# Layer 1 of a recommendation tower: the second pair of fp32 matmuls replaced by three f32r passes, with ScalarE and GpSimd preparing the operands

## The reference

```python
e = jnp.stack([tbl_0[ids[:, 0]], ..., tbl_31[ids[:, 31]]], axis=1)   # (512, 32, 32)
x0 = prev = e
for W in (filter_0, filter_1):
    z = jnp.einsum('bhd,bmd->bhmd', x0, prev).reshape(b, h * m, d)
    cur = jax.nn.relu(jnp.einsum('bpd,pn->bnd', z, W[0]))            # 128 maps
    prev = cur
    outs.append(cur)
z = jnp.sum(jnp.concatenate(outs, axis=1), axis=-1)                  # (512, 256)
h = jnp.concatenate([z, dense_ctx], axis=1)
h = jnp.maximum(h @ W_top1 + b_top1, 0.0)
h = jnp.maximum(h @ W_top2 + b_top2, 0.0)
y = h @ W_top3
```

## Time and profile before

| | before |
|---|---|
| median of 3 runs | 865.25 us (864.55 to 865.81) |
| the profiled execution's own time | 865.07 us |
| span in its profile | 863.3 us |
| busy: TensorE, VectorE, ScalarE, GpSimd | 854.4, 778.2, 680.4, 655.3 us |
| two fp32 matmuls of layer 1 (L751), instructions | 132 |
| mean granted TensorE clock | 0.992 |

### The profile page before, as it was taken

One profiled execution on the slowest core, in us unless ns is written; L12 is line 12 of the kernel. 1 busy time (PEld: TensorE's weight loads), 2 busy tenths in 40 slices (PEclk: granted clock), 3 DMA queues, 4 the chain that ended last, 5 costly groups with the idle time before them and its releaser, 6 DMA issues.

```text
span 863.3 us, 13937 instructions
## 1 busy us (share of the span) xinstructions
PE 854.4 (99%) x3583; PEld 672.2 (78%) x3583; DVE 778.2 (90%) x2392; ACT 680.4 (79%) x2231; POOL 655.3 (76%) x677
## 2 busy tenths in 40 slices
PE   8999999999999999999999999999999999999998
PEld 3777787777778777777877777787777778777866
DVE  4889999999999999999999999999999999999952
ACT  3778888888888888888888888888888888888832
POOL 5577788888887888778788877778878878866740
PEclk9999999999999999999999999999999999999988
DMA  5878866668677666777666687766668776664500
GB/s 168 200 201 197 199 133 139 158 161 185 163 170 151 135 157 162 182 165 181 146 131 153 162 182 167 178 151 131 150 158 185 168 178 137 139 145 93 99 6 0
DMA packets 54949, 130.86 MB, mean 152 GB/s; under 512 B 8020, under 2 KB 18996, under 8 KB 54869
## 3 DMA queue, kind: packets, MB, share of 16 engines
q0 software_dynamic: 22240, 68.17, 42.9%
q1 hardware_dynamic: 31090, 59.13, 22.4%
q10 hardware_dynamic: 1539, 2.67, 0.9%
HBM read 59.69 MB, written 4.20 MB: 74 GB/s over the span
## 4 chain that ended last, share of the span: by engine, by line
PE 96%; DMA 2%; DVE 1%; POOL 0%; ACT 0%; issue 0%; SPq 0%; ACTq 0%
PE t_act L784 13%; PE t_act L786 13%; PE t_act L785 13%; PE t_dve L784 13%; PE t_dve L786 13%; PE t_dve L785 13%; PE acc L751 7%; PE acc L756 5%; PE t_act L794 1%; PE acc L760 1%; DMA x_rows<-emb 1%; PE t_dve L805 1%; PE t_dve L841 1%; PE t_act L862 0%; PE t_dve L855 0%; DVE prod L577 0%
## 5 line engine op out<-in xcount | busy, mean ns | idle before, releaser
L420 ACT ACTIVATE prod<-t_act,weigh 128x128 f32<-128x128 f32 x2048 | 576.5, 373 | 101.5 <-PE t_act L786 96.6
L577 DVE SCALAR_TENSOR_TENSOR prod<-t_dve,weigh,prod 128x128 f32<-128x128 f32 x1792 | 481.5, 342 | 9.4 <-PE t_dve L786 7.4
L303 POOL TENSOR_TENSOR prod<-prod 128x512 f32<-128x512 f32 (+1 forms) x255 | 296.8, 1164 | 19.6 <-DMA prod<-prod 8.8
L784 PE MATMUL t_act<-w_hi,cur_hi 128*128 128x512 f32 x512 | 212.3, 415 | 0.0
L786 PE MATMUL t_act<-w_hi,cur_lo 128*128 128x512 f32 x512 | 199.7, 390 | 0.0
L785 PE MATMUL t_act<-w_lo,cur_hi 128*128 128x512 f32 x512 | 199.6, 390 | 0.0
L784 PE MATMUL t_dve<-w_hi,cur_hi 128*128 128x512 f32 x512 | 199.5, 390 | 0.0
L786 PE MATMUL t_dve<-w_hi,cur_lo 128*128 128x512 f32 x512 | 199.3, 389 | 0.0
L785 PE MATMUL t_dve<-w_lo,cur_hi 128*128 128x512 f32 x512 | 199.1, 389 | 0.0
L283 POOL DMA_DIRECT2D prod<-prod x126 | 118.9, 944 | 104.6 <-ACT prod L420 63.2
L264 POOL DMA_INDIRECT emb<-table_dram,all_ids x128 | 163.8, 1279 | 40.0 <-issue 30.0
(11 more groups left out here) (93 smaller groups left out, 572.9 us busy)
## 6 DMA issues: line engine op xcount, KB each, us to landing
prod<-prod POOLq DMA_DIRECT2D x126, 512.0 KB, 5.1
x_shift<-x_rows SPq DMA_DIRECT2D x62, 512.0 KB, 5.9
x_pair<-x_rows SPq DMA_DIRECT2D x94, 128.0 KB, 4.3
x_same<-x_rows SPq DMA_DIRECT2D x31, 256.0 KB, 3.3
x_rows<-emb SPq DMA_DIRECT2D x64, 64.0 KB
w_raw<-w_dram ACTq DMA_DIRECT2D x8, 256.0 KB, 4.1
emb<-table_dram,all_ids POOLq DMA_INDIRECT x128, 2.9
w_raw<-wt_dram SPq DMA_DIRECT2D x2, 512.0 KB, 9.9
```

The costliest lines, as they stand in the source:

```text
L303: nc.gpsimd.tensor_tensor(src[:, dst, :], src[:, dst, :], src[:, other, :], ALU.add).then_inc(folded, 1)
L420: last = nc.scalar.activation(prod[i][:, HEADS * a + j, :], t_act[n % ARING][:, j * MAPS:(j + 1) * MAPS], ACT.Copy, scale=weigh[p][:, i, h ...
L577: nc.vector.scalar_tensor_tensor(dst, src, w, dst, ALU.mult, ALU.add).then_inc(added, 1)
L784: nc.tensor.matmul(bank[:, :], cur_hi[p][:, cols], w_hi[:, w], start=True, stop=False)
```

## The change

All four groups of layer 1 are done in three f32r passes from chunk 3 on (chunks 0 to 2 stay as they were). The z_hi, z_lo, v_hi and v_lo buffers have four groups in place of two. For the added groups 0 and 1, ScalarE rounds both in one activation (`round_first`), between `relu2` and tile 3, and `round_last` moves behind tile 3; GpSimd makes the two low parts (`lower_first`), between the fold of tile 1 and `halve` of tile 3. To make room in SBUF, the context input and its weights lie in `w_raw`, and the rounded halves of `pool1` in z_hi and z_lo. A semaphore counts the first half of each layer 1 (`layer1_half`), for which `round_first` waits; two more connect ScalarE, GpSimd and TensorE.

```diff
-SPLIT = 2
-WHOLE = GROUPS - SPLIT
+WHOLE = GROUPS // 2
...
-        z_hi = sb("z_hi", [128, SPLIT, COLS], f32r)
-        z_lo = sb("z_lo", [128, SPLIT, COLS], f32r)
+        z_hi = sb("z_hi", [128, GROUPS, COLS], f32r)
+        z_lo = sb("z_lo", [128, GROUPS, COLS], f32r)
...
-        v_hi = sb("v_hi", [128, SPLIT, MAPS], f32r)
-        v_lo = sb("v_lo", [128, SPLIT, MAPS], f32r)
+        v_hi = sb("v_hi", [128, GROUPS, MAPS], f32r)
+        v_lo = sb("v_lo", [128, GROUPS, MAPS], f32r)
...
-        ctx_sb = sb("ctx_sb", [CTX, BATCH])
-        wt1_ctx = sb("wt1_ctx", [CTX, TOP1])
...
+        room = 2 * TOP1 + T1 * TOP2
+        ctx_sb = w_raw[0:CTX, room:room + BATCH]
+        wt1_ctx = w_raw[0:CTX, room + BATCH:room + BATCH + TOP1]
...
-        pool1_hi, pool1_lo = (sb(f"pool1_{half}", [128, BATCH], f32r)[:, :] for half in ("hi", "lo"))
+        pool1_hi, pool1_lo = z_hi[:, 0, :], z_lo[:, 0, :]
...
+            def lower_first(c, p):
+                pool.wait_ge(first_rounded, c - LEAD + 1)
+                for g in range(WHOLE):
+                    nc.gpsimd.tensor_tensor(z_lo[:, g, :], z[p][:, g, :], z_hi[:, g, :].bitcast(fp32),
+                                            ALU.subtract).then_inc(first_lo_ready, 1)
...
+                    if i == 3 and 0 < c < CHUNKS - 2:
+                        lower_first(c + 2, p)
...
+            def round_first(c, p):
+
+                act.wait_ge(z_ready, c * 3 + 1)
+                act.wait_ge(layer1_half, c - 1)
+                nc.scalar.activation(z_hi[:, 0:WHOLE, :], z[p][:, 0:WHOLE, :], ACT.Copy).then_inc(first_rounded, 1)
...
-                    if i == 2 and not ((c == 0 or c + 2 >= CHUNKS)):
+                    if i == 2 and 0 < c < CHUNKS - 2:
+                        round_first(c + 2, p)
+                    if i == 3 and 0 < c < CHUNKS - 2:
                         round_last(c + 2, p)
...
-            nc.vector.tensor_copy(v_hi[:, :, :], v[:, WHOLE:GROUPS, :]).then_inc(v_ready, 1)
+            nc.vector.tensor_copy(v_hi[:, :, :], v[:, :, :]).then_inc(v_ready, 1)
...
-                    if g < WHOLE or g < GROUPS and c <= 2:
+                    if g < GROUPS and c < LEAD:
...
-                        nc.tensor.matmul(acc1[:, :], v[:, g, :], z[p][:, g, :], start=g == 0, stop=False)
+                        last = nc.tensor.matmul(acc1[:, :], v[:, g, :], z[p][:, g, :], start=g == 0, stop=False)
+                        if g == WHOLE - 1:
+                            last.then_inc(layer1_half, 1)
                     elif g < GROUPS:
-                        k = g - WHOLE
-                        pe.wait_ge(z_lo_ready, (c - 3) * SPLIT + k + 1)
-                        for weights, rows in ((v_hi, z_hi), (v_lo, z_hi), (v_hi, z_lo)):
-                            nc.tensor.matmul(acc1[:, :], weights[:, k, :], rows[:, k, :], start=False, stop=False)
+                        if g < WHOLE:
+                            pe.wait_ge(first_lo_ready, (c - LEAD) * WHOLE + g + 1)
+                        else:
+                            pe.wait_ge(z_lo_ready, (c - LEAD) * WHOLE + g - WHOLE + 1)
+                        nc.tensor.matmul(acc1[:, :], v_hi[:, g, :], z_hi[:, g, :], start=g == 0, stop=False)
+                        nc.tensor.matmul(acc1[:, :], v_lo[:, g, :], z_hi[:, g, :], start=False, stop=False)
+                        last = nc.tensor.matmul(acc1[:, :], v_hi[:, g, :], z_lo[:, g, :], start=False, stop=False)
+                        if g == WHOLE - 1:
+                            last.then_inc(layer1_half, 1)
```

More of the change, by code:

```diff
@@ L147, in dlrm_tower @@
         z_rounded = sem("z_rounded")
+        layer1_half, first_rounded, first_lo_ready = sem("layer1_half"), sem("first_rounded"), sem("first_lo_ready")
         pair_rounded, z_lo_ready = sem("pair_rounded"), sem("z_lo_ready")
@@ L235, in chunk @@
                 sp.dma_start(x_shift[p][:, WHOLE:GROUPS, :].rearrange("p g c -> p (g c)"),
-                             shifted(WHOLE, SPLIT)).then_inc(x_rest[p], 16)
+                             shifted(WHOLE, GROUPS - WHOLE)).then_inc(x_rest[p], 16)
             def top_loads():
@@ L396, in round_pair @@
                 act.wait_ge(layer1_done, c)
-                nc.scalar.activation(z_hi[:, :, :], z[p][:, WHOLE:GROUPS, :], ACT.Copy).then_inc(pair_rounded, 1)
+                nc.scalar.activation(z_hi[:, WHOLE:GROUPS, :], z[p][:, WHOLE:GROUPS, :], ACT.Copy).then_inc(pair_rounded, 1)
             def relu2(c, p):
@@ L528, in lower_pair @@
                 dve.wait_ge(pair_rounded, c - 2)
-                for k in range(SPLIT):
-                    nc.vector.tensor_tensor(z_lo[:, k, :], z[p][:, WHOLE + k, :], z_hi[:, k, :].bitcast(fp32),
+                for g in range(WHOLE, GROUPS):
+                    nc.vector.tensor_tensor(z_lo[:, g, :], z[p][:, g, :], z_hi[:, g, :].bitcast(fp32),
                                             ALU.subtract).then_inc(z_lo_ready, 1)
@@ L608, in _ @@
             dve.wait_ge(v_ready, 1)
-            nc.vector.tensor_copy(v_hi[:, :, :], v[:, WHOLE:GROUPS, :]).then_inc(v_ready, 1)
+            nc.vector.tensor_copy(v_hi[:, :, :], v[:, :, :]).then_inc(v_ready, 1)
             dve.wait_ge(v_ready, 2)
-            nc.vector.tensor_tensor(v_lo[:, :, :], v[:, WHOLE:GROUPS, :], v_hi[:, :, :].bitcast(fp32),
+            nc.vector.tensor_tensor(v_lo[:, :, :], v[:, :, :], v_hi[:, :, :].bitcast(fp32),
                                     ALU.subtract).then_inc(v_ready, 1)
```

## The result

| | before | after |
|---|---|---|
| median | 865.53 us (864.55 to 868.05, 4 runs) | 899.66 us (896.39 to 904.58, 4 runs) |
| the profiled execution's own time | 865.07 us | 899.89 us |
| span in its profile | 863.3 us | 898.1 us |
| busy: TensorE, VectorE, ScalarE, GpSimd | 854.4, 778.2, 680.4, 655.3 us | 857.8, 851.7, 699.1, 776.0 us |

The kernel became slower by the factor 1.0401 (95% interval 1.0358 to 1.0443). The forecast was 911 us, 11 us too much; the time lies in the range of 861 to 933. What follows gives the mechanism as forecast in the main, one of its two reasons refuted, and one engine that had not been counted.

A forecast was written before the change was run, and what follows sets the result against it. TensorE was taken as the bound, with GpSimd to become it: 28 periods of 26.86 instead of 25.14 us add 48.2, less 2.6 of lead, so 865.07 + 45.6 and 0.2 give 911 us; range 861 to 933.

The forecast's parts named there:

- TensorE's part: Layer 1's first half: six f32r passes replace the fp32 pair, 1.36 for 1.72 us, saving 0.36 us per chunk, 10.4 total.
- ScalarE, preamble, addresses at nothing: ScalarE's added 1.07 us rounding, moved round_last, larger v_hi and v_lo, and changed SBUF places were taken to cost nothing.
- it fits: Rival: GpSimd never falls behind and TensorE's saving of 0.36 to 0.41 us per chunk shows, 854.9 to 853.4 us; chance 0.12.
- The first reason, the chain through a landing: GpSimd's path from tile 3's DMA through tile 1's landing, fold and subtractions takes 25.1 us, over TensorE's 24.78.
- bound by the landing chain, but the collisions stay off: Rival: GpSimd's period is 25.1 us and the product stays in the second subtraction, 861.5 us; chance 0.06.
- The second reason, the collisions: VectorE's two-SBUF-input operations and GpSimd's tensor operations block each other, first the product in lower_first; 2.30 us per chunk.
- 24.56 + 2.30 = 26.86 us: GpSimd's period: 22.08 us without waits plus 2.48 for subtractions, then blocks of 1.13, 0.87 and 0.3 us.
- the lead that is used up first: GpSimd's 2.9 us ahead of TensorE's need for low parts, less 0.36, taken off the loss as 2.6 us.
- 28 equal periods: From chunk 3's layer 1 to chunk 31's, each period lengthens from 25.14 to 26.86 us, 48.2 us more.
- no wait of GpSimd for ScalarE or VectorE left: Sign expected in the profile after: GpSimd, late throughout, no longer waits for tiles from ScalarE or VectorE.
- the idle 2.48 us in which the product lay: GpSimd's wait before the DMA at 454.49, where VectorE's 1.13 us product at 453.86 ran and lower_first would stand.

The follow-up runs named there:

- the run with one-input products: Changed kernel with VectorE's three products per chunk replaced by transposes of one input, products left out of the computation: 853.66 us, ratio 0.9847 to the kernel before.
- one subtraction each: Changed kernel with GpSimd making only group 0's low part and VectorE group 1's, between tile 3 and the second product: 876.83 us, ratio 1.0126 to the kernel before.

## Why the prediction was right in its direction, and where it was wrong

**TensorE's part: right.** 0.36 us per chunk, or 0.41 with the slower passes behind the fp32 pair, were forecast; 0.41 was measured (24.73 against 25.14). In the run with one-input products the six passes take 1.36 us, as written. The change gets nothing of it, since TensorE no longer sets the pace.

**ScalarE, preamble, addresses at nothing: right.** The run without GpSimd's subtractions has all of them and ends at 855.77, with 855 forecast for "it fits". In the change the layer 1 of chunk 3 even starts 0.7 us earlier, not later.

**The first reason, the chain through a landing: wrong.** The step "that is 25.1 us around, over 24.78" took 444.13 - 429.36 = 14.77 us for GpSimd's work, and in these stood a gather of 2.11 us. 1.06 of it was a collision with the product beside it, so the chain is 24.0 us. The step should have asked why one gather of four takes twice as long as the others. The rival "bound by the landing chain, but the collisions stay off", 861.5 us, is not what comes without the products' collisions: the period is then TensorE's 24.73. The time of the other branch, "it fits" (854.9 to 853.4), is that of the run with one-input products (853.66). Its condition, a loss below 0.22 us per chunk, was too tight, since the gathers held by z_lo lose 1.1 us in ten chunks of that run, 0.4 per chunk, and cost nothing.

**The second reason, the collisions: right, and the whole of the loss.** Half of the place was wrong, though: the collision at the subtractions is the smaller part, 13.1 of the 46.0 us, and the first product and z_last against the folds are the larger. The product splits the subtraction pair as described, but from chunk 2 on. In chunk 1, where the prediction saw it already, the fold ended at 74.5 and not at the 75.74 of the kernel before, so the product was due in the second subtraction, was held itself, and GpSimd was spared. Both timelines of the change, GpSimd and then VectorE:

```profile
74.50 2.56 POOL L281 TENSOR_TENSOR z_lo<-z,z_hi 128x512 fp32r<-128x512 f32 x2
...
100.65 3.52 POOL L281 TENSOR_TENSOR z_lo<-z,z_hi 128x512 fp32r<-128x512 f32 x2
```

```profile
76.14 2.00 DVE L537 TENSOR_TENSOR z<-x_shift,x_same 128x1024 f32<-128x1024 f32 x1
...
101.24 1.78 DVE L537 TENSOR_TENSOR z<-x_shift,x_same 128x1024 f32<-128x1024 f32 x1
```

**The size: the sum was right by two errors that nearly cancel.** The forecast was 24.56 + 2.30 = 26.86 us for GpSimd's period. Measured, its work is 24.73 - 1.15 = 23.58 us in the chunk of the run with one-input products in which nothing is held, and the collisions are 3.53 - 2.55 = 1.0 in the subtractions, 4.21 - 2.55 = 1.7 in one fold and 2.91 - 2.55 = 0.4 in another, 3.0 in all: 26.6. The distance of the subtractions from 100.65 to 793.26 us, 26 chunks, gives 26.64. So 24.56 held a collision of 1.06 that the kernel before already had, and 2.30 was 0.7 too small: errors of about 1.0 and 0.7 us in opposite directions. That they nearly cancel is luck, and so is much of how close 911 comes. Over 28 periods, with the lead that is used up first, 45.6 us were forecast and 37.5 measured. The lead was right at the start: the low parts of chunk 3 are done at 77.06 us, 2.55 before TensorE starts on that layer 1. But at the end they are still 1.79 us ahead (819.25 against 821.04), so only 0.8 us of it went. What makes the 8.1 us is the period, 26 x 0.22 = 5.7, and its two ends: the first distance between two pairs of subtractions is 26.15 us, and the last, from 793.26 to 816.72, 23.45, since GpSimd has no gathers left in the last of these chunks. The sum had taken 28 equal periods. That is 0.7 + 3.4 + 5.7 - 1.8 = 8.0. The shorter stretches ahead of and behind the 28 periods make the other 2.7 us.

**VectorE: not foreseen.** The prediction counted a collision as a loss of GpSimd's. VectorE loses as much: in the chunk shown cur_lo 1.80, the second product 0.61 and the two z_lo 0.61 us, 3.0 us in all. On average over the 26 chunks VectorE's two-input operations lose 3.2 us per chunk, and GpSimd's subtractions and folds 2.9. VectorE is full at 26.5 of 26.76. The kernel before had 1.4 us of idle time in VectorE's period, less than half of that. TensorE's stall on t_dve banks, 22.6 us in all, is VectorE's lateness. The profile was to show "no wait of GpSimd for ScalarE or VectorE left", and from 95 to 800 us it has one such wait before the DMA of L290, of 0.9 us, and six short ones before gathers, 1.3 us in all: the sign came true there. The other 18 us of the two lines of the waits lie in the first and the last chunks.

**What "it fits" lacked.** Its chance of 0.12 rested on a sum of busy times. Single collisions in the trace before and the idle 2.48 us in which the product lay were what spoke against it, and they did decide.

## What to carry to other kernels

Work that is put into an engine's idle time has to be read against what the other engine does in that very stretch, by which ports it uses, and not by its length: here 2.5 us into a gap of 2.48 us cost 34 us against the kernel before, and 46 against what TensorE would have allowed. 13 of the 46 come from the gap itself, where VectorE's two-input product had run free, and more, 27, from the folds that now meet VectorE elsewhere in the chunk. Before adding to GpSimd, look for operations of one form whose duration differs from their siblings' (a gather of 2.11 us among three of 1.1 on average); these are collisions already being paid, and show what a shift will do. Where both engines are above 90% busy, count each collision on both, and test with a version in which the suspected operation reads one input only, made to the kernel before as well.

## What the runs showed of the hardware that was not expected

- An indirect gather issued by GpSimd is held by a two-input operation of VectorE: 2.11 us beside the product, 2.1 to 2.2 beside two z_lo, 1.05 beside a transpose of 128x1024 of the same length. VectorE's operation keeps its length beside it (1.22 and 0.68). The accumulating DMA of `halve` was held in none of the traces here (0.83 to 1.06 us for each of the 126).
- Memsets of GpSimd and VectorE's product don't disturb each other (0.96 and 1.22 us side by side).
- Who wins is not told by the starts in the profile. With one subtraction each, the product starts at 513.95, 0.06 us before the fold, and takes 2.74 us; in the change cur_lo starts 0.17 us before the fold, and takes 2.48. What waits slips in between two operations of the other engine, however closely they follow: that is how a pair is split.
- The pattern is stable. The 24 split pairs take 3.51 to 3.55 us, and the same operations meet from chunk to chunk. That this is because each collision makes both engines late together fits the two losses of about 3 us, but no run tests it.
